# Attention scores: one VectorE operation over two broadcast rows and one exponential in a four-layer graph network

## The reference

```python
def gat_conv(x, src, dst, W, a_src, a_dst, bias, H, C, n):
    h = (x @ W).reshape(n, H, C)
    s_src = (h * a_src).sum(-1)
    s_dst = (h * a_dst).sum(-1)
    e = jax.nn.leaky_relu(s_src[src] + s_dst[dst], NEG_SLOPE)      # slope 0.2
    emax = jax.ops.segment_max(e, dst, num_segments=n)
    ee = jnp.exp(e - emax[dst])
    denom = jax.ops.segment_sum(ee, dst, num_segments=n)
    alpha = ee / denom[dst]
    out = jax.ops.segment_sum(alpha[:, :, None] * h[src], dst, num_segments=n)
    return out.reshape(n, H * C) + bias
```

## Time and profile before

| | us |
|---|---|
| median of three runs | 4486.59 |
| lowest, highest | 4484.09, 4494.87 |
| profiled execution, first to last instruction | 4488.1 |
| TensorE busy | 3479.2 |
| VectorE busy | 2280.6 |
| ScalarE busy | 1404.6 |
| GpSimd busy | 821.0 |

### The profile page before, as it was taken

The page is one execution under the profiler, slowest core; times in us unless marked ns, Lnnn a source line. Parts: engine busy times, 40 slices in busy tenths (PEclk is TensorE's granted clock), DMA queues, the critical chain, the costliest instruction groups (busy, mean ns, idle before and its releaser), DMA issues. The chain is left out here.

```text
span 4488.1 us, 53210 instructions
## 1 busy us (share of the span) xinstructions
PE 3479.2 (78%) x19962; PEld 3212.7 (72%) x19963; DVE 2280.6 (51%) x3552; ACT 1404.6 (31%) x1882; POOL 821.0 (18%) x626
## 2 busy tenths in 40 slices
PE   8715577667879686775686918999978999969999
PEld 7715466557769585554685707888868999969998
DVE  6736677475423466897666684233223233222332
ACT  2203344242333233432233412222223323323233
POOL 0000244140000031443232002112102122010210
PEclk9956789568879798988798959999988999979999
DMA  0020000003121220000210032121112121121311
GB/s 2 18 107 28 4 1 4 5 22 101 53 69 46 98 75 13 1 0 34 79 44 4 1 110 75 43 71 51 62 59 77 61 84 48 43 99 40 108 54 63
DMA packets 103611, 219.10 MB, mean 49 GB/s; under 512 B 8884, under 2 KB 83073, under 8 KB 101198
## 3 DMA queue, kind: packets, MB, share of 16 engines
q1 hardware_dynamic: 103448, 217.01, 14.3%
HBM read 171.13 MB, written 45.85 MB: 48 GB/s over the span
## 5 line engine op out<-in xcount | busy, mean ns | idle before, releaser
L1414 PE MATMUL psum<-v,g_wgt 125*125 125x256 f32 (+2 forms) x2600 | 564.0, 381 | 180.9 <-DVE g_wgt L1282 167.9
L1414 PEld LDWEIGHTS psum<-v,g_wgt 125*125 125x125 f32 x2600 | 490.3, 211 | 252.4 <-DVE g_wgt L1282 193.0
L847 POOL CAST p_w_hi<-p_w_raw 128x384 fp32r<-128x384 f32 (+3 forms) x248 | 179.1, 722 | 2610.8 <-DMA p_w_raw<-in_L_gnn_w_rel_dram 1293.6
L946 DVE TENSOR_TENSOR p_l_lo<-h_t,p_l_hi 128x750 fp32r<-128x750 f32 (+2 forms) x440 | 482.1, 1102 | 226.3 <-ACT p_l_hi L893 221.6
L1064 PE MATMUL psum<-p_w_hi,p_l_lo 128*125 128x384 f32 (+4 forms) x2844 | 550.5, 333 | 34.4 <-DVE p_l_lo L946 33.5
L1064 PE MATMUL psum<-p_w_lo,p_l_hi 128*125 128x384 f32 (+4 forms) x2844 | 541.2, 330 | 0.0
L1064 PE MATMUL psum<-p_w_hi,p_l_hi 128*125 128x384 f32 (+4 forms) x2844 | 537.9, 328 | 0.0
L893 ACT CAST p_l_hi<-h_t 128x750 fp32r<-128x750 f32 (+2 forms) x440 | 390.9, 893 | 404.5 <-PE psum L1064 331.9
L1064 PEld LDWEIGHTS psum<-p_w_hi,p_l_lo 128*125 128x125 f32 (+1 forms) x2844 | 473.1, 192 | 57.6 <-DVE p_l_lo L946 46.7
L1064 PEld LDWEIGHTS psum<-p_w_lo,p_l_hi 128*125 128x125 f32 (+1 forms) x2844 | 475.0, 192 | 9.2
L1064 PEld LDWEIGHTS psum<-p_w_hi,p_l_hi 128*125 128x125 f32 (+1 forms) x2844 | 472.5, 190 | 9.4
(11 more groups left out here) (174 smaller groups left out, 3879.4 us busy)
## 6 DMA issues: line engine op xcount, KB each, us to landing
p_c<-c_dram SPq DMA_DIRECT2D x18, 3051.8 KB
p_w_raw<-in_L_gnn_w_rel_dram SPq DMA_DIRECT2D x78, 192.0 KB
p_w_raw<-in_L_gnn_w_rel_dram SPq DMA_DIRECT2D x42, 224.0 KB
c_dram<-counts SPq DMA_DIRECT2D x3, 3051.8 KB
res_dram<-p_fin SPq DMA_DIRECT2D x70, 125.0 KB
x_dram<-p_fin SPq DMA_DIRECT2D x40, 187.5 KB
t_rows<-x_dram SPq DMA_DIRECT2D x20, 375.0 KB
act_dram<-p_fin SPq DMA_DIRECT2D x40, 187.5 KB
```

The lines of the kernel that those rows point to most:

```text
L847: pool.tensor_copy(w_hi[0:rows, j % 2, b, :width(j)], raw).then_inc(hi_made, 1)
L946: dve.tensor_tensor(l_lo[0:rows, t % 2, b:b + cnt], src[0:rows, q:q + cnt, t * P:(t + 1) * P], l_hi[0:rows, t % 2, b:b + cnt].bitcast(F32) ...
L1414: ins = pe.matmul(acc(t), w[:, t * P:(t + 1) * P], v[:, b, h, c:c + wide], start=(b == 0 and first), stop=(b == NT - 1), skip_group_check= ...
```

## The change

In all four stages the score is now made in one way. DVE adds the column s_high to d_row0 and takes the larger of this and d_row1, in one scalar_tensor_tensor (the new function `scores`); ACT takes one exponential with the bias s_low; DVE makes the weight. Row 0 now holds d minus the maximum in every stage. The relu on ACT, the addition on POOL, the second exponential and DVE's maximum are gone. In `weights` DVE does the scores of block m + 1 before it waits for the exponential of block m. At the start of a new head these scores need rows that aren't there yet, so they come after the last `prepare`, ahead of the first weight of the new head. ACT's queue is the exponentials in order, with the row copies after the third and the tenth of a head.

```diff
@@ gpsimd
                 if ones_col:
                     pool.memset(v[:, :, :, ch:], 1.0).then_inc(ones_set, 1)
-                    for m in range(NT * len(passes)):
-                        h = passes[m // NT][0]
-                        pool.wait_ge(relus, m + 1)
-                        pool.tensor_tensor(e1[:, m % NE], e1[:, m % NE], d_row[:, h % 2, 1], ALU.add).then_inc(larger, 1)
@@ vector, shifts
-                    if ones_col:
-                        dve.tensor_scalar(shift[:, 0], d_col[:, h], 1.0 - SLOPE, None, ALU.mult)
-                    else:
-                        dve.tensor_tensor(shift[:, 0], d_col[:, h], most[:], ALU.subtract)
+                    dve.tensor_tensor(shift[:, 0], d_col[:, h], most[:], ALU.subtract)
@@ vector
+                def scores(m):
+
+                    h, b = passes[m // NT][0], m % NT
+                    if b == 0:
+                        dve.wait_ge(row_out, 3 * (3 * h + 3))
+                    if m >= NE:
+                        dve.wait_ge(exps, m - NE + 1)
+                    dve.scalar_tensor_tensor(e1[:, m % NE], d_row[:, h % 2, 0], s_high[:, h, b:b + 1], d_row[:, h % 2, 1],
+                                             ALU.add, ALU.max).then_inc(larger, 1)
+
                 def weights(p, b):
-                    h, m = passes[p][0], NT * p + b
-                    dve.wait_ge(exps, (1 if ones_col else 2) * (m + 1))
-                    if not ones_col:
-                        dve.tensor_tensor(e1[:, m % NE], e1[:, m % NE], e2[:, m % NE], ALU.max).then_inc(larger, 1)
+                    m = NT * p + b
+                    if m + 1 < NT * len(passes) and (b + 1 < NT or not new_head(p + 1)):
+                        scores(m + 1)
+                    dve.wait_ge(exps, m + 1)
...
-                    if not ones_col:
-                        dve.wait_ge(larger, m + 1)
-                    e = e2 if ones_col else e1
-
-                    dve.scalar_tensor_tensor(wgt[:, m % NW], e[:, m % NE], 1.0, k.ctot[:, b], ALU.min,
+                    dve.scalar_tensor_tensor(wgt[:, m % NW], e2[:, m % NE], 1.0, k.ctot[:, b], ALU.min,
                                              ALU.mult).then_inc(weighed, 1)
...
+                scores(0)
                 for p, (h, c) in enumerate(passes):
...
                     if p + 1 < len(passes):
-
+                        if new_head(p + 1):
+                            scores(NT * (p + 1))
                         weights(p + 1, 0)
                     reduce(p)
@@ scalar
-                def relu_of(m):
...
-                def two_exponentials(m):
...
                 for m in range(NT * len(passes)):
                     p, b = divmod(m, NT)
-                    if ones_col:
-
-                        relu_of(m)
-                        if m:
-                            exponential(m - 1)
-                    else:
-                        two_exponentials(m)
+                    exponential(m)
                     if new_head(p + 1):
                         prepare(passes[p + 1][0], b)
-                if ones_col:
-                    exponential(NT * len(passes) - 1)
```

More of the change, by code:

```diff
@@ L1149, in attention @@
         s_low = sb("s_low", [P, heads, NT], F32)
-        s_high = sb("s_high", [P, heads, NT], F32) if ones_col else None
+        s_high = sb("s_high", [P, heads, NT], F32)
         top = sb("top", [P, NT], F32)
@@ L1171, in attention @@
         topped = sem("topped")
-        relus = sem("relus")
         exps = sem("exps")
@@ L1308, in _ @@
                 dve.tensor_scalar(s_low[:], s_col, SLOPE, None, ALU.mult).then_inc(cols_made, 1)
-                if ones_col:
-                    dve.tensor_scalar(s_high[:], s_col, 1.0 - SLOPE, None, ALU.mult).then_inc(cols_made, 1)
+                dve.tensor_scalar(s_high[:], s_col, 1.0 - SLOPE, None, ALU.mult).then_inc(cols_made, 1)
+                dve.wait_ge(cols_made, 2)
                 for b in range(NT):
                     prepare(0, b)
+                scores(0)
                 for p, (h, c) in enumerate(passes):
@@ L1355, in exponential @@
                     act.activation(e2[:, m % NE], e1[:, m % NE], ACT.Exp, bias=s_low[:, h, b:b + 1]).then_inc(exps, 1)
-                def two_exponentials(m):
[L1358 to L1366, removed]
+                act.wait_ge(cols_made, 2)
                 for b in range(NT):
```

## The result

| | before | after |
|---|---|---|
| median, us | 4490.73 (4 runs, 4484.09 to 4495.41) | 4419.06 (4 runs, 4411.15 to 4422.24) |
| profiled execution, span | 4488.1 | 4409.2 |
| mean granted TensorE clock | 0.872 | 0.877 |

The ratio is 0.9839, 95% interval 0.9824 to 0.9853: 72 us less. The prediction was 4410, range 4394 to 4434. The two profiled executions differ by 78.9.

A forecast was written before the change was run, and what follows sets the result against it. DVE was taken to bound most heads, taking turns with POOL in g0 and g1; PE paced g0's last. Gains of g0 41.6, g1 26.9, g2 5.7, g3 2.7 sum to 76.9, off the median 4486.6: about 4410, range 4394 to 4434.

The forecast's parts named there:

- POOL's turn, 2.2 an addition: In g0 and g1, DVE and POOL take turns, so each of 60 POOL additions costs DVE about 2.2 us.
- The head that prepares the next, 55.2: Two g0 heads: 42.8 us on DVE plus 12.4 at the end, 55.2 each; gain 23.1 for both.
- T: The end of a head's diagonals on DVE; from there to the next reciprocals PE sets the time in g0, 12.4 us.
- First head of g0, 58.7: From rows ready to reciprocals: 58.7 us instead of 76.5, with about 3 waiting for s_row; gain 17.8.
- Last head, 37.8: g0's last head, paced by PE: 6.6 us, then nine blocks of 3.44; 37.8 instead of 38.5, gain 0.7.
- g1, 26.9: Gain in stage g1: first head 55.2 us, gain 20.7; second head 28.5, set by DVE, gain 6.2.
- g2, 5.7: Gain in stage g2, from DVE's self-wait (4.1), late row copies (-1.8), start (2.4) and last head's end (about 1).
- (a): The new scores operation is slow on DVE: gain gone at 2.14 us, kernel 4543 at half rate; 3 in 100.
- (b): Head ends cost more: seven, each losing 3 us more than allowed, gives 4431; 12 in 100.
- (c): PE stays at 1.2 GHz in g0's preparing heads, which then gain nothing: about 4451; 4 in 100.
- (d): In g2 and g3 POOL's turn moves, 50 blocks lose or gain 0.3 us each: 4395 or 4425; 8 in 100.
- (e): More gain at head ends and in cold heads, clock up earlier: 2 us in each of eight, 4394; 10 in 100.

The follow-up runs named there:

- e3: Against before: in g0 and g1 the addition moves from POOL to DVE and the relu stays on ACT; 4444.63 us, ratio 0.9891.
- e4: After's kernel plus one POOL addition per scores operation of g0 and g1, reading and writing a tile nobody else uses; 4494.84 us.
- e5: After's kernel plus two write-only POOL memsets per scores operation of g0 and g1, on a tile nobody else uses; 4422.51 us.
- e1: The change in g0 and g1 only, g2 and g3 keeping the old way; 4420.36 us, ratio 0.9845 to before.
- e6: After's kernel with ACT's copy of the next head's first d row ahead of the tenth block's exponential; 4410.66 us, ratio 0.9834 to before.
- e7: After's kernel with the sums of the weights in g2 and g3 made on DVE instead of POOL; 4389.05 us, ratio 0.9784.
- e8: After's kernel with both the earlier row copy and the sums of the weights on DVE; 4387.39 us, ratio 0.9777 to before.
- e10: After's kernel with constant 0 in place of the column s_high in the scores operation; 4408.62 us.

## Why the prediction was right, and where it was off

**POOL's turn, 2.2 an addition: right in kind, high in sum.** e3, e4 and e5 show the turns from three sides, and without the additions every DVE operation in g0 and g1 has its short length. But the turns lengthened DVE's operations by 110 in all, 1.8 an addition, and that is only part of what leaving POOL brings: the larger part of the gain, 42 of 66.3, is waits of DVE that went. The forecast was not hurt by this, because its sum never uses the 2.2: it takes before's heads as measured and counts the new ones from their operations.

**The head that prepares the next, 55.2: right, 55.5 and 55.8.** The scores have a pitch of 1.43, not the 1.37 I took (the weight's): seven blocks on DVE, 0.4 a head. I had named longer scores rows as a sign of being wrong; they are longer, by 0.06, inside the upper end of 1.5, which I priced at 13 over 100 blocks. 0.06 a block is 6. From T to the reciprocals I had 12.4; the row says 12.4, with PE's sums at T + 5.7 instead of T + 5.3 and the rows at T + 6.3 instead of about T + 6.

**First head of g0, 58.7: 58.3.** The wait for `s_row` was 2.09, not about 3. **Last head, 37.8: 36.4.** The clock is 1.00 there. PE's blocks take 3.29 (28.91 for 176 products in one row), not the 3.44 that I read from the earlier trace rows. That row mixes two paces. While POOL worked, DVE's weights of 3.65 set the pace of this head before the change, and PE's blocks were 3.56 apart, as the row ahead of it shows; only the last ones came at 3.29. So this head was not PE's before, and the change gained 2.1 in it, not 0.7. My sum had a slip too: 6.6 + 9 x 3.44 is 37.6. The timeline of PE in that head, before:

```profile
735.20 10.68 PE L1414 MATMUL psum<-v,g_wgt 125*125 125x193 f32 x60 [0.49 <-DVE g_wgt L1282]
```

and after:

```profile
689.68 28.91 PE L1389 MATMUL psum<-v,g_wgt 125*125 125x193 f32 x176
```

That g0 as a whole meets 41.6 with 42.5 is in part this head's 1.4 making up for the 1.0 that the two preparing heads gained less.

**g1, 26.9: 23.8, the largest miss.** First head, 56.5 instead of 55.2: about 0.5 is the column's pitch, and 0.8 the end, 11.3 from T instead of 10.5. PE's products for the rows took longer, DVE got the rows at T + 7.1 (874.55 to 881.65) and from there set the end itself. PE and DVE after, at that head's end:

```profile
875.57 5.59 PE L1368 MATMUL psum<-g_diag,ones 125*125 125x500 f32 x12
...
881.65 2.95 DVE L1265 SCALAR_TENSOR_TENSOR g_e<-g_d_row,g_s_high 125x1250 f32<-125x1250 f32 x2 [2.71 <-ACT g_d_row L1332]
...
885.95 0.26 DVE L1290 RECIPROCAL g_rden<-psum 125x5 f32<-125x5 f32 x2
```

Second head, 30.4 instead of 28.5: I had DVE set it, with PE at 2.4 a block. The windows of after in that head (columns as above):

```profile
888.00:903.00 15.00, 15.00 (x79) 14.86 (x78) 15.00 (x14) 6.69 (x5) 0.00 (x0) 0.54 0.00 0
903.00:916.00 13.00, 13.00 (x122) 13.00 (x121) 9.46 (x7) 4.02 (x3) 0.00 (x0) 1.00 0.00 1
```

For 15 us PE ran mostly at 1.2 GHz, 79 products without a break, 3.8 a block against DVE's 2.8, and it needed the whole head to catch up; so PE set the end. This is that execution's: in e1, e5, e6, e7 and e8, with the same code in g1, the head took 29.7, so the clock is worth 0.7 of the 1.9. In e10 the same stretch had 0.94:

```profile
884.00:897.00 13.00, 11.75 (x93) 11.09 (x93) 13.00 (x11) 6.69 (x5) 0.00 (x0) 0.94 0.00 0
```

and the head took 29.3, the scores being 8 x 0.06 = 0.5 shorter. That this is still above 28.5 is an error of my own: the last two weights come 1.37 apart, and PE has two blocks left to do behind them, 4.61 from the first of the two, where I counted one of 2.4 from the second. PE in e10:

```profile
905.07 4.61 PE L1389 MATMUL psum<-v,g_wgt 125*125 125x97 f32 x40 [0.32 <-DVE g_wgt L1280]
```

I had called the clock in g1 the least sure term, at up to 4 us.

**g2, 5.7: 4.4; g3, 2.7: 3.3.** The start is as predicted, 2.45 in each stage where I had 2.4. The timeline after, start of g2:

```profile
1733.83 1.28 ACT L1347 ACT_TABLE_LOAD   x1
1733.84 2.95 DVE L1265 SCALAR_TENSOR_TENSOR g_e<-g_d_row,g_s_high 125x1250 f32<-125x1250 f32 x2 [6.32 <-ACT g_d_row L1332]
1735.40 2.77 ACT L1347 ACTIVATE g_e<-g_e,g_s_low 125x1250 f32<-125x1250 f32 x2 [0.29 <-DVE g_e L1265]
1736.77 1.46 DVE L1280 SCALAR_TENSOR_TENSOR g_wgt<-g_e,ctot 125x1250 f32<-125x1250 f32 x1
```

The load is hidden beside the scores, the exponential starts 0.29 behind its end and 0.05 behind the scores', and the first weight comes 2.96 after the rows instead of 5.4. The Trainium skill ("ScalarE: Activation LUTs", section "What ACT_TABLE_LOAD costs") counts a drain of 1.38 more; no run here shows it.

The end of g2's last head is right as well, 0.9 for 1, and so is the price of the late row copies: from T to the reciprocals the three head ends took 17.13, 17.13 and 17.29 instead of 16.34, 16.10 and 17.23, 1.9 more for the 1.8 predicted. The missing 1.3 is in the term of 4.1, the wait of DVE for itself between maximum and weight. From the first weight, or the last reciprocals, to T the three heads took 57.34, 59.10 and 59.11 instead of 58.25, 60.13 and 60.12, which is 2.95. A block became 0.15 to 0.17 shorter (in the preparing heads 7.97 instead of 8.14, in the last one 4.98 instead of 5.13), not 0.21, since the column takes 0.06 back; over 19.5 blocks that is 1.2. e10 agrees: without the column these stretches are another 0.37 shorter each.

In g3 the first pass gained 1.9, the start's 2.45 less 0.5 for nine blocks of 0.06. The prediction gave the later passes nothing, but the second gained 1.3: PE, which sets it, took 44.95 instead of 46.23 for its 200 products, at a granted clock of 0.96 instead of 0.93. So that the stage comes out near its 2.7 is partly luck, and 0.3 of the 2.7 had no term behind it in the first place.

**The rivals.** (a) fell with the scores' 1.51; (b), dearer head ends: beyond what I had priced, g1's 0.8 is the only one of note, and moving the copy ahead in e6 takes 4.5 off the seven, 0.6 each; (c) did not happen in g0, whose clock rose, and did in g1, for some 1 to 2 us; (d) fell: the blocks of g2 became 0.15 to 0.17 shorter, not 0.3 either way; of (e), a clock that is up earlier, the 1.3 of g3's second pass is what is seen.

**The total**, 4410 predicted against a median of 4419, is off by 9. The stages account for 3 of it (74.0 for 76.9, with misses of +0.9, -3.1, -1.3 and +0.6 that partly cancel). The rest is where the runs lie: before's median is 4.1 higher with the fourth run, and the untouched part of the program moves by more than what is left.

## What to carry to other kernels

If the same VectorE operation takes 1.45 in one place and 3.6 in another and GpSimd is busy only in the second, the GpSimd operation is not free: price it at what VectorE loses (2.2 for an operation that is hit, 1.8 an addition on average here), and compare with doing it on VectorE (1.4 here). Then look at the waits too: they were 42 of the 66 us gained in g0 and g1, and e4 shows the reverse, 100 us of lengthened operations that cost 80. A step taken out of a strict relay is worth something by itself where queues are in order: the relu was three tenths here. Read each stage between fixed marks of its own, since the rest of a long program moves by more than a small change brings, and cut a stage into pieces before explaining a miss of 1 us: DVE's stretch of 59.10 in g2 came back within 0.02 in four other executions, while the head ends behind it went from 17.1 to 18.7.

## What the runs showed of the hardware that I had not expected

- GpSimd reading SBUF holds even tiny VectorE operations: 1.99 us for one of ten elements (0.16 without it). VectorE's drains from PSUM with one SBUF row kept their 0.41 beside it.
- A scalar column instead of a constant costs scalar_tensor_tensor 0.06 us at 1250 elements (1.51 and 1.45).
- VectorE's wait for its own last operation costs 0.12 here (1.55 between starts instead of 1.43).
